# Token routing and the expert network in one stage, with the first groups planned after three of the four routing turns

## The reference, cut to what matters

```python
x_flat = x.reshape(-1, dim)                       # 4096 tokens, normalised, 256 channels
gate_logits = x_flat @ gate_w.T                   # 8 experts
topk_vals, topk_idx = jax.lax.top_k(gate_logits, 2)
topk_w = jax.nn.softmax(topk_vals, axis=-1)
...
for e in range(E):
    h = jax.nn.gelu(x_flat @ w1[e].T + b1[e], approximate=False)   # 1024 hidden
    y = h @ w2[e].T + b2[e]
    out = out + comb[:, e:e + 1] * y
```

## Time and profile before

| | |
|---|---|
| median of 3 runs | 1518.46 us (1515.61 to 1528.12) |
| profiled execution | 1515.95 us |
| its span, first to last instruction | 1514.2 us |
| mean granted TensorE clock | 0.902 |
| PE busy over the span | 1208.0 us (80%) |
| POOL busy over the span | 489.8 us (32%) |

### The profile page before, as it was taken

How to read it: one execution, slowest core, us unless ns; L and a number is a source line. 1 busy time by engine, 2 the same in 40 slices (tenths; PEclk the granted TensorE clock), 3 DMA queues, 4 the chain that set the end, 5 groups by cost and what they waited for, 6 DMA issues and landing times. The chain is left out here.

```text
span 1514.2 us, 27643 instructions
## 1 busy us (share of the span) xinstructions
PE 1208.0 (80%) x9325; PEld 817.5 (54%) x9326; DVE 761.9 (50%) x1458; ACT 691.7 (46%) x1318; POOL 489.8 (32%) x411
## 2 busy tenths in 40 slices
PE   3979998753988798879879885430999999999992
PEld 2546666521334334433443344420788888888882
DVE  4855655445564666556664445522344444444541
ACT  3565544355667566657756632210323323233221
POOL 3886554112800460061000000764123323232231
PEclk9989999966999999989999995555999999999996
DMA  4755979725600840091034008994333343343326
GB/s 167 180 126 140 195 171 204 154 62 103 177 1 0 169 138 1 21 183 48 1 65 76 1 14 200 258 275 138 69 53 53 44 55 47 50 56 42 55 35 229
DMA packets 330995, 153.67 MB, mean 101 GB/s; under 512 B 282144, under 2 KB 318240, under 8 KB 330784
## 3 DMA queue, kind: packets, MB, share of 16 engines
q1 hardware_dynamic: 297376, 94.84, 30.3%
q0 software_dynamic: 25184, 56.64, 15.8%
q10 hardware_dynamic: 8352, 1.08, 0.5%
...
## 5 line engine op out<-in xcount | busy, mean ns | idle before, releaser
L2100 ACT ACTIVATE moe_hid<-moe_hbank,moe_b1T 128x256 f32<-128x256 f32 x312 | 130.3, 471 | 265.4 <-PE moe_hbank L2057 265.4
L2057 PE MATMUL moe_hbank<-moe_xT,l_w1T 128*128 128x256 f16 x1872 | 212.1, 274 | 37.8 <-DMA moe_xT<-rows_scratch 36.3
L2036 POOL DMA_INDIRECT acc_scratch<-moe_y,moe_meta x78 | 121.9, 1563 | 310.9 <-DVE moe_y L2127 288.2
L2057 PEld LDWEIGHTS moe_hbank<-moe_xT,l_w1T 128*128 x1872 | 183.7, 98 | 59.9 <-issue 38.1
L2072 PE MATMUL moe_ybank<-l_w2T,moe_hid_hi 128*128 x1248 | 206.4, 273 | 0.3 <-DVE moe_hid_lo L2114 0.3
L1139 ACT ACTIVATE block_probs<-block_bank 128x1024 f32<-128x1024 f32 (+1 forms) x192 | 144.5, 808 | 75.5 <-PE block_bank L901 63.1
L2072 PE MATMUL moe_ybank<-l_w2T,moe_hid_lo 128*128 x624 | 170.1, 273 | 0.0
L2112 DVE TENSOR_SCALAR moe_hid_hi<-moe_hid 128x2048 f16<-128x2048 f32 x39 | 47.8, 1226 | 210.1 <-ACT moe_hid L2100 210.1
L898 PE MATMUL block_bank<-block_qkT 128*128 128x512 f16 (+3 forms) x384 | 95.3, 336 | 47.3 <-issue 24.3
L2072 PEld LDWEIGHTS moe_ybank<-l_w2T,moe_hid_hi 128*128 128x128 f16 x1248 | 122.1, 98 | 14.7 <-issue 0.6
L795 POOL COPY block_stack<-block_stack 128x512 f16<-128x512 f16 x16 | 10.6, 661 | 363.6 <-ACT block_stack L1123 363.6
...
## 6 DMA issues: line engine op xcount, KB each, us to landing
...
route_tok<-acc_scratch SPq DMA_DIRECT2D x4, 1024.0 KB, 8.7
```

The costliest lines, as they stand in the source:

```text
L2036: pool.indirect_dma_start(acc, bass.IndirectOffsetOnAxis(ap=meta[r][:, t, 0:1].bitcast(U32), axis=0), y[r % 2][:, t, :], None, compute_op= ...
L2057: last = pe.matmul(hbank[:, c, :], w1T[:, e, wp, k, c * P:(c + 1) * P], xT[q][:, xp * CC + k, :], start=n == 0, stop=n == 5)
L2100: act.activation(hid[q][:, c, :], hbank[:, c, :], ACT.Gelu, bias=b1T[:, e, c:c + 1], scale=1.0 / (GAIN * GAIN)).then_inc(S["gelu_done"], 1)
```

## The change

`route` and `experts` become one block, `route_and_experts`, so the barrier between them is gone. After turn 2 (the third) PE counts the tokens so far, and DVE plans the first 17 groups out of blocks that are already full (`early_groups`, `EARLY_GROUPS` is 17); it signals `planned` once. After turn 3 it plans the other 22 (`late_groups`) and signals `planned` again. The written-out groups 0, 1 and 2 wait for the first signal, and the loop, which begins with group 3, for the second.

SP loads rows for groups 0 and 1 once the scatters of turns 0 to 2 have landed, then writes the tails, then loads group 2, then waits for all scatters and goes on. Buffers are shared: the fourth token buffer is the first, loaded behind the first expert's weights; the hidden halves lie in the token buffers and the first row buffer; `y` lies in the second row buffer, so it waits for the last scatter of turn 3, and the bias sum and the scaling now both work in `y`, so the wait for earlier adds (`added`) stands ahead of the bias sum. The three small PSUM tiles of the routing lie in `hbank`. ACT loads the bias tables behind turn 1.

```diff
-def route(nc, t2, rows, ident, gate_w, w1_parts, w2_parts, w1T, w2T, w_loaded, expert_of, block_of):
+EARLY_TURNS = 3
+EARLY_GROUPS = (EARLY_TURNS * TILES // TURNS * P * TOPK - E_N * (GS - 1) - 1) // GS + 1
+
+
+def route_and_experts(nc, acc, rows, ident, gate_w, w1_parts, w2_parts, b1, b2, w1T, w2T, w_loaded, expert_of, block_of):
...
+        s = Scope(nc, ctx, "moe")
+        shared = s.sb("shared", [P, 3 * PER * D + PER * ROW // 2])
+        tok = [shared[:, i * PER * D:(i + 1) * PER * D].rearrange("p (t d) -> p t d", t=PER) for i in range(3)]
+        tok.append(tok[0])
+        ends = s.sb("ends", [P, PER, ROW], F16)
+        xrow = [shared[:, 3 * PER * D:].bitcast(F16).rearrange("p (t r) -> p t r", t=PER), ends]
+        halves = shared[:, 2 * HC * GS:4 * HC * GS].bitcast(F16).rearrange("p (n c q) -> p n c q", n=4, c=HC)
+        hid = [shared[:, i * HC * GS:(i + 1) * HC * GS].rearrange("p (c q) -> p c q", c=HC) for i in range(2)]
+        hid_hi, hid_lo = [halves[:, i, :, :] for i in range(2)], [halves[:, 2 + i, :, :] for i in range(2)]
+        y = [ends[:, :, :].rearrange("p t r -> p (t r)").bitcast(F32)[:, i * GT * D:(i + 1) * GT * D].rearrange("p (t d) -> p t d", t=GT) for i in range(2)]
...
+        hbank = s.ps("hbank", [P, HC, GS])
+        ybank = [s.ps(f"ybank{i}", [P, GT, D]) for i in range(2)]
         xbank = [s.ps(f"xbank{i}", [P, 512]) for i in range(2)]
-        lbank = s.ps("lbank", [P, PER, E_N])
-        pbank = s.ps("pbank", [P, PER, E_N])
-        cbank = s.ps("cbank", [P, E_N])
-        names = ("consts", "gate_loaded", "tok0", "tok1", "tok2", "tok3",
...
+        def later_tiles(eng, step):
+
+            eng.wait_ge(S["planned"], 2)
+            with eng.Fori(0, (GROUPS - 3) // 4) as i:
+                for r in range(4):
+                    step(i * 4 + (3 + r), (3 + r) % 4)
+
+        assert (GROUPS - 3) % 4 == 0
+
...
                                          allow_slow_non_contiguous=True).then_inc(S["gate_loaded"], 16)
                 for e in range(E_N):
+                    if e == 1:
+                        sp.wait_ge(S["x_lo"], 1)
+                        sp.wait_ge(S["xT_full"], PER)
+                        sp.dma_start(tok[3][:, :, :], t2_v[3]).then_inc(S["tok3"], 16)
                     for part in range(2):
                         sp.dma_start_transpose(w1T[:, e, part, :, :], w1_parts[part, e]).then_inc(w_loaded, 16)
                         sp.dma_start_transpose(w2T[:, e, part, :, :], w2_parts[part, e]).then_inc(w_loaded, 16)
-                sp.wait_ge(S["blank_ready"], 1)
-                sp.dma_start(rows[(BLOCKS - 1) * GS:BLOCKS * GS, :].rearrange("(t p) r -> p t r", p=P), blank[:, :, :].bitcast(U32)).then_inc(S["filled"], 16)
-                sp.wait_ge(S["tail_known"], 1)
-                for e in range(E_N):
-                    at = sp.value_load(tail_at[0:1, e:e + 1], min_val=0, max_val=(BLOCKS - 2) * GS)
-                    sp.dma_start(rows[bass.ds(at, GS), :].rearrange("(t p) r -> p t r", p=P), blank[:, :, :].bitcast(U32)).then_inc(S["filled"], 16)
-                sp.wait_ge(S["filled"], 16 * (E_N + 1))
+                def step(j, r):
+                    if not early(j, 2):
+                        sp.wait_ge(S["h_full"], (j - 1) * (HC // 2))
+                    at = sp.value_load(block_of[0:1, bass.ds(j, 1)], min_val=0, max_val=BLOCKS - 1)
+                    sp.dma_start_transpose(rowT[r % 2][:, :, :], split_v[at]).then_inc(S[f"xT{r % 2}"], 16)
+                    if not early(j, 4):
+                        sp.wait_ge(S["added"], (j - 3) * (16 * GT))
+                    sp.dma_start(meta[r][:, :, :], meta_v[at]).then_inc(S[f"meta{r}"], 16)
+
+                def tails():
+                    sp.wait_ge(S["blank_ready"], 1)
+                    sp.dma_start(rows[(BLOCKS - 1) * GS:BLOCKS * GS, :].rearrange("(t p) r -> p t r", p=P), blank[:, :, :].bitcast(U32)).then_inc(S["filled"], 16)
+                    sp.wait_ge(S["tail_known"], 1)
+                    for e in range(E_N):
+                        at = sp.value_load(tail_at[0:1, e:e + 1], min_val=0, max_val=(BLOCKS - 2) * GS)
+                        sp.dma_start(rows[bass.ds(at, GS), :].rearrange("(t p) r -> p t r", p=P), blank[:, :, :].bitcast(U32)).then_inc(S["filled"], 16)
+                    sp.wait_ge(S["filled"], 16 * (E_N + 1))
+
+                sp.wait_ge(S["planned"], 1)
+                sp.wait_ge(S["second"], EARLY_TURNS * PER * 16)
+                step(0, 0)
+                step(1, 1)
+                tails()
+                step(2, 2)
+                sp.wait_ge(S["second"], TURNS * PER * 16)
+                later_tiles(sp, step)
...
+                            last = pe.transpose(xbank[i % 2][:, k * P:(k + 1) * P], tok[a][:, i, k * P:(k + 1) * P], ident[:, :])
+                        last.then_inc(S["xT_full"], 1)
+                        if i:
+                            logits(a, i - 1)
+                    logits(a, PER - 1)
+                    places(a)
+                    if a + 1 == EARLY_TURNS:
+                        pe.wait_ge(S["sofar_done"], EARLY_TURNS)
+                        pe.matmul(cbank, all_ones[:, :], sofar[:, EARLY_TURNS, :], start=True, stop=True).then_inc(S["counted"], 1)
...
+                        down(j - 1, (r - 1) % 4)
+
+                pe.wait_ge(S["planned"], 1)
+                pe.wait_ge(S["based"], TURNS)
+                pe.wait_ge(S["kept"], 2)
+                pe.wait_ge(w_loaded, 16 * 4 * E_N)
+                all_tiles(pe, step)
+                down(GROUPS - 1, (GROUPS - 1) % 4)
 
...
-                pe.wait_ge(S["sofar_done"], TURNS)
-                pe.matmul(cbank[:, :], all_ones[:, :], sofar[:, TURNS, :], start=True, stop=True).then_inc(S["counted"], 1)
+                    if a == 1:
+                        act.dma_start(b1T[:, :, :], b1.rearrange("e (c p) -> p e c", p=P), allow_slow_non_contiguous=True).then_inc(S["bias_loaded"], 16)
+                        act.dma_start(b2r[:, :, :], b2.rearrange("(a e) d -> a e d", a=1).to_broadcast((P, E_N, D))).then_inc(S["bias_loaded"], 16)
+
+                act.wait_ge(S["planned"], 1)
+                act.wait_ge(S["x_lo"], TURNS)
+                act.wait_ge(S["second"], (TURNS - 1) * PER * 16)
+                act.wait_ge(S["bias_loaded"], 32)
+
+                def step(j, r):
+                    q = r % 2
+                    e = act.value_load(expert_of[0:1, bass.ds(j, 1)], min_val=0, max_val=E_N - 1)
+                    if not early(j, 2):
+                        act.wait_ge(S["lo_done"], j - 1)
+                    for c in range(HC):
...
+                def early_groups():
+                    group_counts(1, full_e, iota_full, ALU.is_ge)
+                    upto = running_sum(full_e)
+                    n = at[0]
+                    dve.tensor_scalar(rest_e[:, :], full_e[:, :], -1.0, float(REGION + 1), ALU.mult, ALU.add).then_inc(plan, 1)
+                    dve.tensor_tensor(room[:, :], full_e[:, :], upto, ALU.subtract).then_inc(plan, 1)
+                    dve.wait_ge(plan, n + 2)
+                    dve.tensor_scalar(more_e[:, :], room[:, :], float(EARLY_GROUPS), 0.0, ALU.add, ALU.max).then_inc(plan, 1)
+                    dve.wait_ge(plan, n + 3)
+                    dve.tensor_tensor(taken[:, :], more_e[:, :], full_e[:, :], ALU.min).then_inc(plan, 1)
+                    at[0] = n + 4
+                    dve.wait_ge(plan, at[0])
+                    assign(0, EARLY_GROUPS, upto, rest_e, 0.0)
+
+                def late_groups():
+                    group_counts(2, groups_e, iota_t, ALU.is_gt)
+                    n = at[0]
+                    dve.tensor_tensor(tail_f[:, :], count[:, :], base_e[:, :], ALU.add).then_inc(plan, 1)
+                    dve.wait_ge(plan, n + 1)
+                    dve.tensor_copy(tail_at[:, :], tail_f[0:1, :]).then_inc(S["tail_known"], 1)
+                    dve.tensor_tensor(more_e[:, :], groups_e[:, :], taken[:, :], ALU.subtract).then_inc(plan, 1)
+                    at[0] = n + 2
+                    upto = running_sum(more_e)
...
+                        dve.wait_ge(S["numbered"], 1)
+                        early_groups()
+                        dve.sem_inc(S["planned"], 1)
+
+                late_groups()
                 dve.wait_ge(S["pos_done"], TURNS)
-
...
@@ -2117,14 +2184,16 @@
                     q = r % 2
                     e = dve.value_load(expert_of[0:1, bass.ds(j, 1)], min_val=0, max_val=E_N - 1)
                     dve.wait_ge(S["y_full"], j + 1)
-                    dve.scalar_tensor_tensor(ysum[q][:, :, :], ybank[q][:, :, :], 1.0 / (GAIN * HID_GAIN),
+                    if not early(j, 2):
+                        dve.wait_ge(S["added"], (j - 1) * (16 * GT))
+                    elif j == 0:
+                        dve.wait_ge(S["second"], TURNS * PER * 16)
+                    dve.scalar_tensor_tensor(y[q][:, :, :], ybank[q][:, :, :], 1.0 / (GAIN * HID_GAIN),
```

(4 more changed lines are left out.)

332 lines of the change are left out of this document (153 added, 179 removed).

## The result

The changed kernel takes 1508.84 us in the median of 20 runs (1500.9 to 1521.11), the kernel before 1520.07 on the same chip (20 runs): ratio 0.991, interval 0.9891 to 0.993. I had forecast 28. The profiled execution took 1509.2 us with a span of 1507.4.

What follows compares the result with a forecast made beforehand. PE bounds the expert stage; before it PE idles 35 us behind turn 3's places, 20 us of scatters, a 6 us block edge and a 5.6 us load. up(3) moves from 1091.0 to 1063.1: 1515.95 - 27.9 = 1488.0, range 1479 to 1501.

Steps and rivals of the forecast that it cites:

- PE's start, 1033.9: Start of up(0): group 0's rows, loaded behind the weights, let PE start at 1033.9, with 1027.6 as the other end.
- the 6.3 us from b1T's packets: Weight loads: the two bias loads, 7.6 us of all engines at share 1.21, push the weights back 6.3 us (bounds 0, 6.3).
- the 145.9: Forecast time from the first token load (917.25) to up(3) (1063.1), the first matmul of the loop: 145.9 us.
- Hidden unless the issue stretches beyond 20 us: ACT behind turn 1: issuing both biases (5.65 us and some 0.5) is hidden by 14.69 us of idle before turn 2's x_hi.
- 17.7 us from up(0) to up(2): PE's first groups: 19.2 us before, less 1.5 us of waiting for biases now loaded early, gives 17.7 us.
- the late plan hidden: DVE after turn 3's count: the plan (1026.60 to 1031.84 before) is done before DVE's split(0), which follows up(0), so costs nothing.
- The saving's base: Start of the loop in the kernel before: up(3) at 1091.0, from up(2) at 1080.51 plus 10.49 us per group.
- Group 2 behind the tails: SP loads group 2 after the tails land, at 1051 to 1053; PE waits 1 us before up(2), bounds 0 and 4.
- the shared y: Loop: the bias sum waits for earlier adds, free with 13 us of slack; as slower rival 43 us, 1531, chance 0.04.
- turn 3 slips: Rival in the routing's last turn: late signals grow by 10 us, up(3) at 1066 to 1073, total 1491 to 1503; chance 0.22.
- No overlap: Rival at the early groups: PE does not get ahead of the last scatters, only 7 us saved, 1509; chance 0.06.
- The fit in its section Anatomy of one DMA: Bias loads: about 2 us plus bytes over 436 GB/s would make the delay 2 us, the sum 4 us lower; not used.

Runs made afterwards that it cites:

- A: Batches of runs, on chip 5 and one unnumbered chip, in which the kernel before had a median of 1520 to 1524 us.
- e5: The changed kernel run again unaltered, on A: 1508.23 us, ratio 0.9881 to the kernel before.
- e13: The changed kernel run a third time unaltered, on A: 1509.62 us, ratio 0.9898 to the kernel before.
- e6: The changed kernel with b1T loaded as 64 rows of 512 bytes and turned by PE, on A: 1502.35 us, ratio 0.9837 to the kernel before.
- e16: The version of e6 (b1T in 64 rows) run again on A: 1507.37 us, ratio 0.9906 to the kernel before.
- e15: The version of e6 with POOL's turn 3 scatters held back until up(1) is through, on A: 1503.69 us, one run.
- B: Batches of runs, on chips 8, 1 and 9, in which the kernel before had a median of 1508 to 1511 us.
- e18: The changed kernel run unaltered on B, chip 9: 1495.17 us, ratio 0.9929 to the kernel before.
- e1: The changed kernel with ACT's two bias loads moved to the head of its code, on B: 1499.13 us, ratio 0.9936 to the kernel before.
- e3: The changed kernel with SP waiting for the second plan signal and all scatters before group 0, on B: 1507.73 us, ratio 0.998 to the kernel before.
- e4: The changed kernel with b1T loaded in 256-byte rows, output not the reference's, on B: 1491.25 us, ratio 0.9901 to the kernel before.
- e12: The version of e6 (b1T in 64 rows) run on B, chip 1: 1490.46 us, ratio 0.9857 to the kernel before.
- e9: The version of e12 with SP loading group 2 without waiting for the tails to land, on B: 1491.38 us, ratio 0.9889 to the kernel before.

## Why the prediction was wrong

**PE's start, 1033.9: met on A, but its term is not shown.** That is 116.7 us after the first load. Measured 118.3 (after), 118.4 (e5), 121.3 (e13). The end of the last weight issue was forecast at 110.8 and came at 110.2, 113.1 and 110.3. But I had the 6.3 us from b1T's packets, in the 0.5% of the earlier trace rows. With b1T in 64 rows (e6) the queue shows

```profile
q10 hardware_dynamic: 224, 1.08, 0.2%
```

which by the same sum is 2.5 us, and still the last weight issue started no earlier on A: 105.6, 112.8 and 109.5 (e6, e16, e15) against 106.4, 110.2 and 107.5. The number came out and what it was worked out from did not: that was luck. On B the term was far too small: up(0) at 130.3, because the last weight was issued at 121.6, behind a single issue held for 13.18 us. That is about the 13.4 us by which e18's up(3), 159.3, misses the 145.9. A share of the engines' time says nothing of it.

**"Hidden unless the issue stretches beyond 20 us": it was hidden, and turn 2 was late all the same.** b2r's issue took 9.86 us, and x_hi came at 57.35 against 58.40 before, so the cover of 14.69 us held. On A the lateness came behind x_hi, in the six copies. In e6, whose b2r is issued in 0.60 us, they crept as well, so it was not the length of the issue:

```profile
990.72 0.38 ACT L1966 ACTIVATE moe_xT<-moe_xbank 128x256 f32<-128x256 f32 x1 [4.62 <-remote]
997.84 0.38 ACT L1966 ACTIVATE moe_xT<-moe_xbank 128x256 f32<-128x256 f32 x1 [6.74 <-remote]
```

In the three traces of before, with no bias load there, the six copies take 5.9 us each time, and waits without releaser fall in other places. Whether a bias load draws them to this one stays open.

On B x_hi itself was late by 9 us and more (66.05 in e18, 66.26 in e1, 69.04 in e3, against 56 to 58 elsewhere on B), but with ACT idle ahead of it for 14.63 to 17.87 us. What I had left out there is that the load of single elements delays others' transfers, here the landing of turn 0's scatters. With b1T in rows b2r's issue is 0.45 to 0.72 us on A and B.

**17.7 us from up(0) to up(2), the late plan hidden: this step failed on A.** It took 33.8 us, and the late plan 26.9 instead of the 5.2 that I took from before. The forecast has 1063.1 - 1033.9 = 29.2 us from up(0) to up(3). In the first trace after it took 44.3, in e18 29.0, in e4 28.5. The 15.1 us on A, with the 1.6 by which PE started late, are the missing 16.7. The crawl lengthens the time between instructions and not their own: the plan's last one takes 0.17 us in both traces. I had priced the plan and the first matmuls at the pace of the one trace of before, and B keeps that pace beside the same scatters. What makes the crawl stays open.

**The saving's base was itself disturbed.** The earlier trace rows showed 5.24 and 17.15 us of late signals in turn 3, and my rival left their cause open. They are A's waits without releaser: turn 3's count comes at 109.4, 100.2 and 97.7 in the three traces of before on A. On B, where it comes at 92.8, before has none, and its up(3) comes 12.6 us earlier in the traces. The forecast's own timeline for the changed kernel, 145.9, was met within 2.3 us by e4, e12 and e9 (143.8, 146.6, 143.6), on B and with b1T in rows. But their mean of 144.7 is only 16.4 us under the 161.1 of before there.

**The rest held.** Group 2 behind the tails cost PE 0.24 us in e4, 0.88 in the first trace after and 2.00 in e5, against the 1 I had counted (0 to 4). The loop ran on as forecast: from up(3) to the end of the span 423.8 us after, 423.2 before, so the shared y cost nothing. The rival *turn 3 slips* named the late signals, which is the nearest that the prediction came to the crawl, and gave 1491 to 1503; the delay was in turn 2 and behind turn 3, and turn 3 itself (logits at 1019.42, 1.19 us behind PE) was not slow. *No overlap* at 1509 has the measured number and not the mechanism: PE worked on groups 0 and 1 beside the scatters, at half speed.

On 512 bytes: the Trainium skill, "DMA: Bandwidth & Descriptors", Specifications, gives 512 bytes as the least transfer for full rate. I named the rule and let it change no term of the sum. The runs agree with its direction (181 against 279 GB/s), though rows of 256 bytes (e4) did as well here as rows of 512 (e12). The fit in its section Anatomy of one DMA, which the prediction quotes from the Trainium skill, is given there for GpSimd's path, and both bias loads went over ScalarE's queue.
